# First attention layer: the norms of the first two batches by Sqrt on ScalarE and reciprocal on VectorE instead of powers on GpSimd, and the padded keys cleared by VectorE at the start

## The chip, the core and the metric

The kernel runs on one NeuronCore of one Trainium2 chip. The metric is the device time of one execution in microseconds (us); lower is better. TensorE (PE) multiplies matrices, ScalarE (ACT) evaluates activation functions, VectorE (DVE) and GpSimd (POOL) work elementwise, SyncE (SP) issues most of the transfers. Each engine runs its own instructions strictly in the order in which they were written down, and waits on semaphores for the others.

## What is computed

Four layers over a tensor x of 16 batches x 256 tokens x 128 features, each with its own layer norms and residual: an attention, a mixture of 8 experts, a second attention, and a mixture of 16 experts. The change touches the first attention alone. Cut to what matters:

```python
def _l2norm(x):                               # EPS_NORM = 1e-12
    n = jnp.linalg.norm(x, axis=-1, keepdims=True)
    return x / jnp.maximum(n, EPS_NORM)

x = layernorm(x) * ln_w + ln_b                # after an outer layernorm
q = _l2norm((x @ Wq + bq).reshape(B, S, 16, 8))
k = _l2norm((x @ Wk + bk).reshape(B, S, 16, 8))
v = (x @ Wv + bv).reshape(B, S, 16, 8)
state = q
for _ in range(2):
    sim = jnp.einsum('bqhd,bkhd->bqhk', state, k)
    state = jnp.einsum('bqhk,bkhd->bqhd', softmax(sim), v)
o = state.reshape(B, S, H) @ Wo + bo
return residual + o
```

The norm is taken over the 8 features of a head. With 128 tokens to a tile, 2 tiles to a batch, 16 heads, and q and k, a batch has 64 norms on each of the 128 partitions.

## The kernel before

`first_attention` is a software pipeline over steps k from -12 to 74. A unit is one group of four heads of one batch, so a batch b has the four units 4b to 4b+3, and 64 units make up the layer. In the code b is k // 4 and r is k % 4. Every engine's block walks through the same steps, and in each step writes down its share for several batches at once, each at another stage. Nothing schedules this but the order in the code and the semaphores. For one batch n the stages are these:

- k = 4n - 12 (r 0, b = n - 3): statistics of X on VectorE (`stats`, L617, and `moments`, L623), then their inverse root on GpSimd (`rstd` into `rs_a`: an addition at L801 and a power at L803).
- k = 4n - 11: the first normalisation into Z on VectorE (L604), the statistics of Z, and `rstd` again into `rs_b`.
- k = 4n - 10: the second normalisation into `z1` on VectorE (L604), its transposes on TensorE (L429), and `xT` on ScalarE (L575).
- k = 4n - 9 (r 3): the three projections of q, k and v on TensorE (L435, into two PSUM banks in turn), read on VectorE at L629 into `qk` and `vt`, and the squares `sq` (L736). On the same step `scaled` = `qk` times the inverse norms is made for the batch before (L671, in front of the reads), and ScalarE casts it into `qt` and `kt` (L565, L567).
- k = 4n - 8 (r 0): the sums of squares `ss` on VectorE (L705), the lower clip at 1e-24 on GpSimd (L852), and two of four powers of -0.5 on GpSimd into `rn` (`norm_powers`, L807, 16 of the 64 columns each).
- k = 4n - 7 (r 1): the other two powers, behind `rstd` of the next batch.
- k = 4n - 4 (r 0): GpSimd subtracts the rounded parts (L838, L840), which releases `stacks_ready`, and the steps 4n - 4 to 4n - 1 each transpose one unit's keys and queries (L423, task "KQ") and ScalarE copies them into `kq` (L590).
- k = 4n: the first unit of the batch is scored (L398), exponentiated on ScalarE (L539, two instructions of 128x1024 a step), and from step 4n + 1 on attended (L416), turned (L522), and worked on in VectorE for the second iteration, with row maxima (L409 on TensorE, L645 on VectorE).

So before step 0 there is nothing but this preparation of batches 0, 1 and 2, and from step 0 on the attention of one unit a step, beside the preparation of later batches.

`kpad`, a ring of four padded key tiles (128x4096 in all), is cleared once by GpSimd in step -6 (L865, at `FIRST + 6`). SyncE waits for that (`kpad_zero`) before its first small transfers into `kpad`, which also need the first copy into `kq`; the maxima first read `kpad` in step 3.

Of the kernel before, what the change touches and what calls it, by code (L numbers as in the profile page):

```python
# [16 lines left out]
F32 = mybir.dt.float32  # L17
F32R = mybir.dt.float32r
I32, U32 = mybir.dt.int32, mybir.dt.uint32
ALU = mybir.AluOpType  # L20
ACT = mybir.ActivationFunctionType
AX = mybir.AxisListType
# [3 lines left out]
B, S = 16, 256  # L26
TILES = B * S // P
TPB = S // P
H, HD = 16, 8
# [164 lines left out]
def first_attention(nc, X, Z, ident, a):  # L194
# [3 lines left out]
    FIRST, LAST = -3 * NG, UNITS + 3 * NG - 1  # L198
# [2 lines left out]
    D_ORDER = ("op", "m0", "qp", "m1", "m2", "lg", "place", "m3", "kp", "vp", "O")  # L201
    PEAK, TURN, SECOND, LAST_USE = 3, 4, 5, 6
    K_RING, Q_RING, PAD_RING, V_RING = NG + LAST_USE, NG + 1, 4, NG + LAST_USE + 1

    def steps(eng):
        for k in range(FIRST, LAST):
# [9 lines left out]
    def unit(n):  # L216
        return 0 <= n < UNITS

    def batch(n):
        return 0 <= n < B  # L220

    with ExitStack() as ctx:
# [6 lines left out]
        def sem(name):  # L229
            return ctx.enter_context(nc.semaphore("a0_" + name))  # L230
# [4 lines left out]
        sq = sb("sq", [P, 2, TPB, D])  # L235
        scaled = sb("scaled", [P, 2, TPB, D])
        ss = sb("ss", [P, 2 * TPB * H])
        rn = sb("rn", [P, 2 * TPB * H])
# [20 lines left out]
        kpad = sb("kpad", [P, PAD_RING, G, S], F32R)  # L259
# [22 lines left out]
        squares, norms, clipped, rn_ready = sem("squares"), sem("norms"), sem("clipped"), sem("rn_ready")  # L282
# [4 lines left out]
        set_up, pool_set_up, kpad_zero = sem("set_up"), sem("pool_set_up"), sem("kpad_zero")  # L287
        passed = a["passed"]
        route = sem("route")
        block = ctx.enter_context(nc.Block())  # L290


# [239 lines left out]
        def _(act):  # L532
# [15 lines left out]
            for st in steps(act):  # L548
                k = st.k
                b, r = k // NG, k % NG  # L550
                if unit(k):
                    exps(st, 0, k, p1)
                if a_live(k, "yT"):
# [40 lines left out]
        def _(dve):  # L594
            nc.vector.memset(mv_a[:, :, :], 1.0).then_inc(set_up, 1)
            nc.vector.memset(mv_b[:, :, :], 1.0).then_inc(set_up, 1)
            nc.vector.memset(qt2[:].rearrange("p a b c -> p (a b c)").bitcast(F32), 0.0).then_inc(set_up, 1)
            dve.wait_ge(set_up, 3)
            dve.wait_ge(a["loaded"], 16 * a["loads"])

# [32 lines left out]
            for st in steps(dve):  # L633
                k = st.k
# [12 lines left out]
                                            ALU.max, negate=True).then_inc(d_done, 1)  # L647


                if r == 3 and batch(b - 2):  # L650

                    dve.wait_ge(d_full, d_count(k, "op"))
                    dve.wait_ge(zb_ready, b - 1)
                    nc.vector.tensor_tensor(y[:].rearrange("p t d -> p (t d)"), narrow(k, "op"), Z[:, tiles(st, -2)],
                                            ALU.add).then_inc(d_done, 1)
# [41 lines left out]
                if r == 1 and batch(b - 3):  # L697
# [1 line left out]
                    dve.wait_ge(x_part, b - 2)  # L699
                    xx = X[:, tiles(st, -3)]  # L700
                    nc.vector.tensor_tensor(xx, xx, y[:].rearrange("p t d -> p (t d)"), ALU.add).then_inc(x_new, 1)
                if r == 0 and batch(b + 2):

                    dve.wait_ge(squares, b + 3)
                    nc.vector.tensor_reduce(ss[:, :], sq[:].rearrange("p a t (h d) -> p (a t h) d", d=HD), AX.X,  # L705
                                            ALU.add).then_inc(norms, 1)
# [84 lines left out]
        def _(pool):  # L791
# [18 lines left out]
            for st in steps(pool):  # L810
                k = st.k
# [32 lines left out]
                for g, (first, last) in enumerate(GROUPS[:-2]):  # L844
# [2 lines left out]
                        pool.wait_ge(route, ROUTE_SET_UP + ROUTE_LINKS * (g + 1))  # L847
                    if 0 <= part < 2 * (last + 1 - first) * TPB:
                        scatter(nc, Z, rt, first * TPB + part // 2, a["xs"], a["scattered"], (part % 2,))
                if r == 0 and batch(b + 2):  # L850
                    pool.wait_ge(norms, b + 3)
                    nc.gpsimd.tensor_scalar(ss[:, :], ss[:, :], 1e-24, None, ALU.max).then_inc(clipped, 1)  # L852
                    pool.wait_ge(clipped, b + 3)
                if r < 2 and batch(b + 2):
                    norm_powers(2 * r)
                    norm_powers(2 * r + 1)
                if k == FIRST + 3:
# [3 lines left out]
                    nc.gpsimd.memset(v32[:, :, :, :, HD].rearrange("p a b c -> p (a b c)"),  # L861
                                     1.0).then_inc(pool_set_up, 1)
                    pool.wait_ge(pool_set_up, 4)
                if k == FIRST + 6:
                    nc.gpsimd.memset(kpad[:].rearrange("p a b c -> p (a b c)").bitcast(F32), 0.0  # L865
                                     ).then_inc(kpad_zero, 1)


def second_attention(nc, X, Z, ident, a):
# [1601 lines left out]
```

## Time and profile before

| | |
|---|---|
| median of 3 runs | 1584.4 us (1583.03 to 1585.36) |
| the profiled execution | 1585.79 us, its span 1584.0 us |
| granted TensorE clock, mean | 0.934 of full speed |
| TensorE matmul busy | 1346.2 us (85%) |
| VectorE busy | 1132.1 us (71%) |
| ScalarE busy | 963.9 us (61%) |
| GpSimd busy | 771.9 us (49%) |

The span runs from the first to the last instruction of the core. Busy times are sums over all four layers, and matmuls are pipelined, so the share of TensorE says little of any one stretch; the first stretch is looked at by itself in the views that follow. Shapes are partitions x elements per partition.

### The profile page before, as it was taken

The page shows a single profiled execution, that of the slowest core. Times are in us where ns is not written, and L with a number is a line of the kernel's source. Part 1 is how long each engine was busy: PE and PEld are TensorE (multiplying, and loading weights), DVE is VectorE, ACT ScalarE, POOL GpSimd, SP SyncE. Part 2 cuts the span into 40 slices and gives each one's busy share as a digit, 9 for nine tenths or more (in the row PEclk, how much of TensorE's full clock was granted, in tenths as well). Part 3 has the DMA queues.
Part 4 walks back from the last instruction along what each step waited for, and adds up shares of the span by engine and source line. Part 5 has one row for each costly group of instructions (what it writes and reads, how often), then busy time and mean ns, then how long its engine had stood idle before and what let it go on. Part 6 is the DMA issues. An engine that isn't in the chain of part 4 may idle for free. (4 is left out here: it accounts for less than half of the span.)

```text
span 1584.0 us, 34293 instructions
## 1 busy us (share of the span) xinstructions
PE 1346.2 (85%) x12185; PEld 1024.2 (65%) x12185; DVE 1132.1 (71%) x3064; ACT 963.9 (61%) x1493; POOL 771.9 (49%) x976
## 2 busy tenths in 40 slices
PE   1699999999987677999338999899999997699997
PEld 1356666666654466999326777676777774588886
DVE  3378889888776455999636688678777876466766
ACT  0488888888875354777304666667666775343332
POOL 7966666777733344999554333444344321001111
PEclk9999999999998698999758999989999999699999
DMA  6010000111110120222202111111111110000000
GB/s 212 14 24 20 21 21 22 27 31 30 32 34 22 37 64 14 75 72 70 89 23 57 37 43 43 44 42 42 41 40 42 38 41 13 1 1 14 7 14 20
DMA packets 75101, 60.68 MB, mean 38 GB/s; under 512 B 17088, under 2 KB 71104, under 8 KB 74560
## 3 DMA queue, kind: packets, MB, share of 16 engines
q1 hardware_dynamic: 70848, 50.21, 11.8%
q0 software_dynamic: 4096, 8.40, 1.7%
q8 instruction: 95, 1.56, 0.4%
q14 instruction: 62, 0.51, 0.1%
HBM read 20.01 MB, written 13.37 MB: 21 GB/s over the span
## 5 line engine op out<-in xcount | busy, mean ns | idle before, releaser
L539 ACT ACTIVATE a_p<-a_ps_s 128x1024 f32<-128x1024 f32 x256 | 258.6, 1032 | 25.6 <-PE a_ps_s L398 23.0
L1263 DVE TENSOR_REDUCE a_qt<-a_ps_d 128x2 fp32r<-128x512 f32 x256 | 174.0, 690 | 73.8 <-PE a_ps_d L1062 40.6
L645 DVE TENSOR_REDUCE a_qt<-a_ps_d 128x2 fp32r<-128x512 f32 x256 | 174.7, 688 | 46.5 <-PE a_ps_d L409 40.3
L807 POOL TENSOR_TENSOR a_rn<-a_ss,a_half 128x16 f32<-128x16 f32 x64 | 186.1, 2924 | 1.5
L1062 PE MATMUL a_ps_d<-a_kpad,a_qs 128*128 128x512 f32 x256 | 126.4, 496 | 27.7 <-DVE a_qt L1263 19.7
L1175 ACT ACTIVATE a_pg<-a_ps_s 128x1024 f32<-128x1024 f32 x128 | 125.9, 1026 | 30.7 <-PE a_ps_s L1051 29.1
L416 PE MATMUL a_ps_o<-a_p,a_v 128*32 128x256 f32 x2048 | 129.3, 392 | 3.7 <-ACT a_p L539 3.7
L409 PE MATMUL a_ps_d<-a_kpad,a_qs 128*128 128x512 f32 x256 | 126.7, 495 | 3.1 <-DVE a_qt L645 2.3
L2195 ACT ACTIVATE f_s<-f_ps_g 128x512 f32<-128x512 f32 x72 | 43.0, 599 | 97.4 <-PE f_ps_g L2133 89.1
L416 PEld LDWEIGHTS a_ps_o<-a_p,a_v 128*32 128x32 f32 x2048 | 61.0, 112 | 53.3 <-issue 22.5
L1040 PE MATMUL a_ps_a<-ident,a_qt 128*128 128x128 f32 x512 | 84.8, 292 | 2.7 <-ACT a_kc L1193 1.2
L1958 DVE TENSOR_TENSOR f_sl<-f_s,f_sh 128x512 fp32r<-128x512 f32 x78 | 77.9, 1038 | 8.9 <-ACT f_sh L1846 8.9
L1062 PEld LDWEIGHTS a_ps_d<-a_kpad,a_qs 128*128 128x128 f32 x256 | 48.3, 190 | 54.6 <-DVE a_qt L1263 23.2
L190 POOL DMA_INDIRECT xs<-Z,r_at x64 | 68.2, 1066 | 24.2 <-issue 15.5
L1197 ACT CAST a_qsm<-a_ps_a 128x512 fp32r<-128x512 f32 x64 | 37.6, 587 | 62.5 <-PE a_ps_a L1040 62.5
L409 PEld LDWEIGHTS a_ps_d<-a_kpad,a_qs 128*128 128x128 f32 x256 | 48.1, 188 | 39.1 <-issue 11.6
L1040 PEld LDWEIGHTS a_ps_a<-ident,a_qt 128*128 128x128 f32 x512 | 66.5, 151 | 8.3 <-issue 6.5
L1452 POOL DMA_INDIRECT a_picked<-ys,rows x64 | 62.8, 981 | 17.7 <-issue 17.7
L1112 PE MATMUL a_ps_o<-a_pg,a_v 128*32 128x256 f32 x1024 | 68.5, 385 | 0.4 <-ACT a_pw L1201 0.4
L2244 DVE TENSOR_TENSOR f_p<-f_h,f_ps_x 128x512 f32<-128x512 f32 x64 | 43.8, 685 | 34.3 <-PE f_ps_x L2105 33.2
L2118 PEld LDWEIGHTS f_ps_y<-wd,f_p 128*128 128x128 f32 x512 | 65.3, 191 | 4.1 <-DVE f_p L2244 0.4
L2118 PE MATMUL f_ps_y<-wd,f_p 128*128 128x128 f32 x512 | 66.3, 275 | 0.2 <-DVE f_p L2244 0.2
(353 smaller groups left out, 3913.6 us busy)
## 6 DMA issues: line engine op xcount, KB each, us to landing
a_kpad<-a_kc SPq DMA_DIRECT2D x512, 32.0 KB
a_kpad<-a_kq SPq DMA_DIRECT2D x256, 32.0 KB, 1.8
f_xin<-xs SPq DMA_DIRECT2D x39, 128.0 KB, 2.1
ys<-f_yout SPq DMA_DIRECT2D x39, 128.0 KB, 2.1
w<-in_w SPq DMA_DIRECT2D x2, 2304.0 KB, 11.4
out_x<-X SPq DMA_DIRECT2D x8, 256.0 KB, 2.3
xs<-f_zero SPq DMA_DIRECT2D x15, 128.0 KB
wgu<-in_wgu SPq DMA_DIRECT2D x1, 1152.0 KB, 5.7
```

The costliest lines, as they stand in the source:

```text
L409: nc.tensor.matmul(bank(st.k, f"m{part}")[:, :], qs2[:, (st.k - 1) % 2, t * P:(t + 1) * P], kpad[:, u % PAD_RING, 2 * c:2 * c + 2, :].rear ...
L416: last = nc.tensor.matmul(ps_o[SLOT * j:SLOT * (j + 1), half * S:(half + 1) * S], v32[:, u % V_RING, t, j, :], probs[:, u % 2, j, t, :], s ...
L539: nc.scalar.activation(probs[:, u % 2, 2 * c:2 * c + 2, :, :].rearrange("p a b c -> p (a b c)"), ps_s[:, 2 * c:2 * c + 2, :].rearrange("p ...
L645: nc.vector.tensor_reduce(qt2[:, (k - PEAK) % 4, 2 * part:2 * part + 2, SHIFT], bank(k, f"m{part}")[:, :].rearrange("p (a b) -> p a b", b= ...
L807: nc.gpsimd.tensor_tensor(rn[:, part * c:(part + 1) * c], ss[:, part * c:(part + 1) * c], half[:, 0:c], ALU.pow).then_inc(rn_ready, 1)
L1040: last = nc.tensor.transpose(ps_a[:, n:n + P], stacked(src[:, (u // NG) % 2, kind, t * H + t0:t * H + t0 + G, :]), ident[:, :])
L1062: nc.tensor.matmul(bank(k, f"m{part}")[:, :], qs[:, k % 2, t * P:(t + 1) * P], kpad[:, k % PAD_RING, GLOBAL, 2 * c:2 * c + 2, :].rearrange ...
L1112: nc.tensor.matmul(ps_o[SLOT * j:SLOT * (j + 1), 0:S], v32[:, u % V_RING, t, j, :], pg[:, u % 2, j, t, :], start=t == 0, stop=t == TPB - 1)
L1175: nc.scalar.activation(pg[:, u % 2, 2 * c:2 * c + 2, :, :].rearrange("p a b c -> p (a b c)"), ps_s[:, 2 * c:2 * c + 2, :].rearrange("p a b ...
L1263: nc.vector.tensor_reduce(qt[:, b % 2, GLOBAL, n:n + 2, SHIFT], bank(k, f"m{part}")[:, :].rearrange("p (j s) -> p j s", s=S), AX.X, ALU.ma ...
L1958: nc.vector.tensor_tensor(sl[:, half_of(n, h)], s[:, half_of(n, h)], sh[:, half_of(n, h)].bitcast(F32), ALU.subtract).then_inc(sl_done, 1)
L2118: last = nc.tensor.matmul(ps_y[:, t * D:(t + 1) * D], src, a["wd"][:, q * D:(q + 1) * D], start=q == 0 and t == 0, stop=q == NQ - 1 and t ...
```

## The change

A constant `ROOTED = 2` names how many batches take the new way. For batches 0 and 1:

- VectorE makes the sums of squares at the very front of step 4n - 8 (before, they stood behind the statistics of the next batch), and clips them itself.
- ScalarE takes the square root in the same step, in place in `ss`.
- VectorE takes the reciprocal into `rn` at the front of step 4n - 7, and adds 4 to `rn_ready` at once.
- GpSimd does neither the clip nor the four powers.

Batches 2 to 15 keep the powers. Besides, `kpad` is cleared by VectorE in its set-up, behind the memset of `qt2`, and no longer by GpSimd.

```diff
+    ROOTED = 2
...
+        roots = sem("roots")
...
             for st in steps(act):
                 k = st.k
                 b, r = k // NG, k % NG
+                if r == 0 and 0 <= b + 2 < ROOTED:
+                    act.wait_ge(clipped, b + 3)
+                    nc.scalar.activation(ss[:, :], ss[:, :], ACT.Sqrt).then_inc(roots, 1)
                 if unit(k):
                     exps(st, 0, k, p1)
...
             nc.vector.memset(qt2[:].rearrange("p a b c -> p (a b c)").bitcast(F32), 0.0).then_inc(set_up, 1)
+            nc.vector.memset(kpad[:].rearrange("p a b c -> p (a b c)").bitcast(F32), 0.0).then_inc(kpad_zero, 1)
             dve.wait_ge(set_up, 3)
...
+                if r == 0 and 0 <= b + 2 < ROOTED:
+                    dve.wait_ge(squares, b + 3)
+                    nc.vector.tensor_reduce(ss[:, :], sq[:].rearrange("p a t (h d) -> p (a t h) d", d=HD), AX.X,
+                                            ALU.add).then_inc(norms, 1)
+                    dve.wait_ge(norms, b + 3)
+                    nc.vector.tensor_scalar(ss[:, :], ss[:, :], 1e-24, None, ALU.max).then_inc(clipped, 1)
+                if r == 1 and 0 <= b + 2 < ROOTED:
+                    dve.wait_ge(roots, b + 3)
+                    nc.vector.reciprocal(rn[:, :], ss[:, :]).then_inc(rn_ready, 4)
                 if r == 3 and batch(b - 2):
...
-                if r == 0 and batch(b + 2):
+                if r == 0 and ROOTED <= b + 2 < B:
 
                     dve.wait_ge(squares, b + 3)
...
-                if r == 0 and batch(b + 2):
+                if r == 0 and ROOTED <= b + 2 < B:
                     pool.wait_ge(norms, b + 3)
...
-                if r < 2 and batch(b + 2):
+                if r < 2 and ROOTED <= b + 2 < B:
                     norm_powers(2 * r)
                     norm_powers(2 * r + 1)
...
-                if k == FIRST + 6:
-                    nc.gpsimd.memset(kpad[:].rearrange("p a b c -> p (a b c)").bitcast(F32), 0.0
-                                     ).then_inc(kpad_zero, 1)
```

How the order of the instructions changes, at three places. The line numbers of the changed kernel are a little higher than those of the kernel before; the tiles are the same, named a_ for this layer.

GpSimd, from step -8 to step -4, before:

```order
L852 TENSOR_SCALAR a_ss<-a_ss 128x64 [waits a0_norms]
L807 TENSOR_TENSOR a_rn<-a_ss,a_half 128x16 [waits a0_clipped]
L807 TENSOR_TENSOR a_rn<-a_ss,a_half 128x16
L801 TENSOR_SCALAR a_ve<-a_mv_b 128x4 [waits a0_stats_b]
L803 TENSOR_TENSOR a_rs_b<-a_ve,a_half 128x4 [waits a0_pool_ve]
L807 TENSOR_TENSOR a_rn<-a_ss,a_half 128x16 x2
L865 MEMSET a_kpad 128x4096
L833 TENSOR_TENSOR Z<-Z,bo 128x256 [waits a0_z1_ready]
L824 COPY a_v<-a_vt 128x8x8 [waits a0_d_done]
L838 TENSOR_TENSOR a_qt<-a_scaled,a_qt 128x32x8 [waits a0_parts_hi]
L840 TENSOR_TENSOR a_kt<-a_scaled,a_kt 128x32x8
```

and with the change, from the same `rstd` of batch 1 (the power into `rs_a`) to the same end:

```order
L818 TENSOR_TENSOR a_rs_a<-a_ve,a_half 128x4 [waits a0_pool_ve]
L816 TENSOR_SCALAR a_ve<-a_mv_b 128x4 [waits a0_stats_b]
L818 TENSOR_TENSOR a_rs_b<-a_ve,a_half 128x4 [waits a0_pool_ve]
L848 TENSOR_TENSOR Z<-Z,bo 128x256 [waits a0_z1_ready]
L839 COPY a_v<-a_vt 128x8x8 [waits a0_d_done]
L853 TENSOR_TENSOR a_qt<-a_scaled,a_qt 128x32x8 [waits a0_parts_hi]
L855 TENSOR_TENSOR a_kt<-a_scaled,a_kt 128x32x8
```

The clip, four powers and the memset are gone, so that the `rstd` into `rs_b` and the subtractions into `qt` and `kt` follow each other directly.

VectorE, the end of step -9 and the steps -8 and -7, before:

```order
L629 TENSOR_TENSOR a_vt<-a_ps_d,bqkv 128x256 [waits a0_d_full]
L617 BN_STATS a_bn<-X 128x6 [waits x_first]
L617 BN_STATS a_bn<-X 128x6
L623 BN_AGGR a_mv_a<-a_bn 128x2 [waits a0_bn_done]
L623 BN_AGGR a_mv_a<-a_bn 128x2
L705 TENSOR_REDUCE a_ss<-a_sq 128x64 [waits a0_squares]
L604 TENSOR_SCALAR Z<-X,a_mv_a,a_rs_a 128x128 [waits a0_rs_a_ready]
```

and with the change:

```order
L635 TENSOR_TENSOR a_vt<-a_ps_d,bqkv 128x256 [waits a0_d_full]
L658 TENSOR_REDUCE a_ss<-a_sq 128x64 [waits a0_squares]
L661 TENSOR_SCALAR a_ss<-a_ss 128x64 [waits a0_norms]
L623 BN_STATS a_bn<-X 128x6 [waits x_first]
L623 BN_STATS a_bn<-X 128x6
L629 BN_AGGR a_mv_a<-a_bn 128x2 [waits a0_bn_done]
L629 BN_AGGR a_mv_a<-a_bn 128x2
L664 RECIPROCAL a_rn<-a_ss 128x64 [waits a0_roots]
L610 TENSOR_SCALAR Z<-X,a_mv_a,a_rs_a 128x128 [waits a0_rs_a_ready]
```

The sums of squares of batch 0 and their clip now stand ahead of the statistics of batch 1, and the reciprocal ahead of its first normalisation. The same pattern comes once more for batches 1 and 2, in steps -4 and -3.

ScalarE, from the first `xT` (step -10) to the Sqrt of batch 1 (step -4), with the change (before, the second load and both rows on `a_ss` are not there):

```order
L580 ACT_TABLE_LOAD [waits a0_a_full]
L580 ACTIVATE a_xT<-a_ps_a,ln_b,ln_w 128x256 [waits loaded]
L555 ACT_TABLE_LOAD
L555 ACTIVATE a_ss<-a_ss 128x64 [waits a0_clipped]
L580 ACTIVATE a_xT<-a_ps_a,ln_b,ln_w 128x256 [waits a0_a_full]
L570 CAST a_qt<-a_scaled 128x32x16 [waits a0_qk_scaled]
L572 CAST a_kt<-a_scaled 128x64x8
L555 ACTIVATE a_ss<-a_ss 128x64 [waits a0_clipped]
```

ScalarE around step 0, before:

```order
L590 CAST a_kq<-a_ps_a 128x2x256 [waits a0_a_full]
L565 CAST a_qt<-a_scaled 128x32x16 [waits a0_qk_scaled]
L567 CAST a_kt<-a_scaled 128x64x8
L590 CAST a_kq<-a_ps_a 128x2x256 [waits a0_a_full]
L539 ACTIVATE a_p<-a_ps_s 128x1024 [waits a0_scores_full] x2
L590 CAST a_kq<-a_ps_a 128x2x256 [waits a0_a_full]
```

and with the change:

```order
L570 CAST a_qt<-a_scaled 128x32x16 [waits a0_qk_scaled]
L572 CAST a_kt<-a_scaled 128x64x8
L595 CAST a_kq<-a_ps_a 128x2x256 [waits a0_a_full]
L541 ACT_TABLE_LOAD
L541 ACTIVATE a_p<-a_ps_s 128x1024 [waits a0_scores_full] x2
L595 CAST a_kq<-a_ps_a 128x2x256 [waits a0_a_full]
```

A table load now stands between the last copy into `kq` of step -1 and the first exponentials. It is the last one in this layer.

## Rows read from the trace of the kernel before

**Rows 1.** Windows: length; busy us (instructions) of PE, PEld, DVE, ACT, POOL; clock; DMA, GB/s.

```profile
30.00:40.00 10.00, 3.69 (x14) 2.71 (x12) 3.78 (x10) 1.71 (x3) 10.00 (x7) 1.00 0.00 0
...
80.00:120.00 40.00, 37.58 (x394) 23.07 (x395) 31.40 (x97) 33.78 (x47) 28.28 (x25) 1.00 0.10 24
```

**Rows 2.** Waits from 0 to 90 us: waiting, releaser, us in total, times, longest.

```profile
DVE a_z L604 <- POOL a_rs_b L803: 17.0, 4, 6.6
```

**Rows 3.** GpSimd's timeline: start, us, line, operation, idle before.

```profile
21.77 5.80 POOL L807 TENSOR_TENSOR a_rn<-a_ss,a_half 128x16 f32<-128x16 f32 x2
...
34.69 3.51 POOL L865 MEMSET a_kpad<- 128x4096 f32 x1
...
39.02 0.72 POOL L838 TENSOR_TENSOR a_qt<-a_scaled,a_qt 128x256 fp32r<-128x256 f32 x1
```

**Rows 4.** VectorE's timeline, the same columns.

```profile
9.11 0.60 DVE L604 TENSOR_SCALAR Z<-X,a_mv_a,a_rs_a 128x128 f32<-128x128 f32 x2 [1.57 <-POOL a_rs_a L803]
...
12.00 0.60 DVE L604 TENSOR_SCALAR a_z<-Z,a_mv_b,a_rs_b 128x128 f32<-128x128 f32 x2 [1.48 <-POOL a_rs_b L803]
...
18.59 0.42 DVE L629 TENSOR_TENSOR a_vt<-a_ps_d,bqkv 128x256 f32<-128x256 f32 x1
...
19.60 0.65 DVE L705 TENSOR_REDUCE a_ss<-a_sq 128x64 f32<-128x512 f32 x1
21.23 0.62 DVE L604 TENSOR_SCALAR Z<-X,a_mv_a,a_rs_a 128x128 f32<-128x128 f32 x2 [0.98 <-POOL a_rs_a L803]
...
29.04 0.60 DVE L604 TENSOR_SCALAR a_z<-Z,a_mv_b,a_rs_b 128x128 f32<-128x128 f32 x2 [6.39 <-POOL a_rs_b L803]
...
49.78 0.60 DVE L604 TENSOR_SCALAR a_z<-Z,a_mv_b,a_rs_b 128x128 f32<-128x128 f32 x2 [6.58 <-POOL a_rs_b L803]
...
58.51 0.42 DVE L629 TENSOR_TENSOR a_vt<-a_ps_d,bqkv 128x256 f32<-128x256 f32 x1 [0.77 <-PE a_ps_d L435]
...
69.08 0.60 DVE L604 TENSOR_SCALAR a_z<-Z,a_mv_b,a_rs_b 128x128 f32<-128x128 f32 x2 [2.54 <-POOL a_rs_b L803]
```

**Rows 5.** TensorE's timeline, the same columns.

```profile
15.41 2.96 PE L435 MATMUL a_ps_d<-wqkv,a_xT 128*128 128x128 f32 x12 [2.00 <-ACT a_xT L575]
...
31.05 2.08 PE L435 MATMUL a_ps_d<-wqkv,a_xT 128*128 128x128 f32 x8 [0.66 <-ACT a_xT L575]
...
40.48 0.69 PE L423 MATMUL a_ps_a<-ident,a_kt 128*128 128x128 f32 x2 [3.28 <-POOL a_kt L840]
...
52.75 1.92 PE L435 MATMUL a_ps_d<-wqkv,a_xT 128*128 128x128 f32 x8
...
57.74 0.63 PE L423 MATMUL a_ps_a<-ident,a_kt 128*128 128x128 f32 x2
...
67.09 1.94 PE L416 MATMUL a_ps_o<-a_p,a_v 128*32 128x256 f32 x16
69.74 0.45 PE L429 MATMUL a_ps_a<-ident,a_z 128*128 128x128 f32 x2 [0.71 <-DVE a_z L604]
```

**Rows 6.** ScalarE's timeline at the first exponentials, the same columns.

```profile
58.84 0.59 ACT L590 CAST a_kq<-a_ps_a 128x512 fp32r<-128x512 f32 x1 [1.45 <-PE a_ps_a L423]
59.59 1.94 ACT L539 ACTIVATE a_p<-a_ps_s 128x1024 f32<-128x1024 f32 x2 [0.16 <-PE a_ps_s L398]
```

**Rows 7.** ScalarE's timeline in the last layer, where the tables change.

```profile
1441.54 1.28 ACT L2202 ACT_TABLE_LOAD   x1
1442.83 0.26 ACT L2202 ACTIVATE f_ex<-f_lg 128x64 f32<-128x64 f32 x1
```

**Rows 8.** VectorE's groups by form: count, busy, mean ns, idle before.

```profile
L1966 DVE RECIPROCAL f_g<-f_den 128x32 f32<-128x32 f32 x1 | 0.4, 352 | 0.0
```

**Rows 9.** VectorE's timeline at the very start: the memset, the first statistics.

```profile
1.09 0.91 DVE L597 MEMSET a_qt<- 128x1024 f32 x1 [0.17 <-issue]
6.77 0.49 DVE L617 BATCH_NORM_STATS2 a_bn<-X 128x6 f32<-128x128 f32 x2 [4.77 <-DMA ln_b<-in_ln_b]
```

**Rows 10.** One window of 1 us, the columns of Rows 1.

```profile
74.00:75.00 1.00, 1.00 (x12) 0.39 (x8) 0.18 (x1) 1.00 (x2) 1.00 (x3) 0.50 0.00 0
```

## The prediction

> **What bounds the kernel now.** I read the windows first, to see where the time is not work. From 30 to 40 us TensorE is busy 3.7 us and GpSimd all 10; from 80 to 120 us TensorE is busy 37.6 of 40 [rows 1]. So the layer has a start in which TensorE mostly waits, and then a steady part in which it is the bound. The inputs are no limit in between: from 30 to 40 us the transfers move nothing (0 GB/s, [rows 1]), so the rest of X has landed before 30. Nothing later depends on a time of its own, so what the start loses, the whole program should lose.
>
> Then the waits up to 90 us: VectorE waits 17.0 us in four times for the inverse roots that GpSimd makes for the second normalisation [rows 2]. GpSimd's timeline shows why: the powers of one batch take 5.8 us a pair, in the same queue as the short `rstd` of the next batch. The `rstd` of batch 1 has to wait until the first pair ends at 27.57 [rows 3], though the statistics that it needs follow the normalisation of 21.23 at once; VectorE idles 6.39 us and normalises at 29.04 [rows 4]. The clearing of `kpad` (3.5 us at 34.69) delays the subtractions of step -4 in the same manner [rows 3]. Each batch of the preparation therefore takes about 20 us: the second normalisations come at 29.04, 49.78 and 69.08, where the reader sees GpSimd named as the releaser each time [rows 4].
>
> TensorE's timeline, last, shows what that does to it: keys are first transposed at 40.48, and the fourth unit's, after which the first scores can be made, at 57.74 [rows 5].
>
> **The change, step by step.** I follow the path with the powers gone, using lags of the same trace where nothing stood in the way. Times are from the span's start.
>
> Unimpeded lags: first to second normalisation, 9.11 to 12.00, is 2.9 us [rows 4]. From the first projection of batch 0 (15.41) to the read of v (18.59) is 3.2 us, and its 12 matmuls take 3.0 without a break [rows 4, 5].
>
> Step A, batch 1 reaches TensorE. VectorE now puts the sums of squares (0.65 us [rows 4]) and the clip (64 columns; I put it at 0.2, a little under the 0.26 of ScalarE's 64 columns [rows 7]) ahead of batch 1's statistics: +0.9. Its first normalisation moves from 21.23 to 22.1, its second comes 2.9 later at 25.0, and no longer at 29.04. That is -4.0 [rows 4].
>
> Step B, batch 0's keys. ScalarE's Sqrt waits for the clip until about 19.9, and all that stands behind it on ScalarE is the next `xT` at 26.4. Its table load carries no wait and runs right after the first `xT`, before 17, where ScalarE has nothing else to do. The reciprocal of 64 columns I estimate at 0.55 us, from 0.35 for 32 columns [rows 8], so the norms stand at 21 and `scaled` no longer waits. The projections start at 27.0 (31.05 less 4.0) and run their 3.0 us through, to 30.0, because both banks are read in time [rows 5]. The two casts behind `xT` (0.6 us each, as the cast into `kq` [rows 6]) end at 28.1, and the two subtractions (0.7 each [rows 3]) at 29.6, since GpSimd has nothing else to do. So the first transposes of keys come at 30.0 and not at 40.48: -10.5 [rows 5]. ScalarE's second Sqrt, in front of the first copy into `kq`, holds that copy about 0.7 us; only the copy and the second transposes feel it, and they have 4 us of slack before the `xT` of batch 2.
>
> Step C, batch 2. v of batch 1 is read from 30.2; 18.59 to 21.23 and the 0.9 make 3.5 us to the first normalisation, 2.9 more to the second: 36.6 and not 49.78, -13.2 [rows 4].
>
> Step D, to the last of the first four transposes. Before, projections began 3.0 after the second normalisation (52.75 against 49.78), then stood while `scaled` waited for the norms, and the transposes came at 57.74 [rows 4, 5]. Now it is 36.6 + 3.0 + 3.0 = 42.5: -15.2. GpSimd's subtractions for batch 1 follow the casts of 40.4 and end at about 43.0, before TensorE asks for them, behind the first scores, at 44.4.
>
> Step E, the table. The exponentials would start at 59.59 - 15.2 = 44.4. Now a table load stands behind the copy into `kq` that ends at 59.43 - 15.2 = 44.2 [rows 6]. In the last layer a load takes 1.28 us and the ACTIVATE follows 0.01 us later [rows 7]. So they start at 45.5: the gain here is 14.1.
>
> Step F, where two paths meet. Batches 2 and 3 still go the old way. v of batch 2 is read 3.2 after its projections start, from 42.8, and was read from 58.51 [rows 4], so all that hangs on GpSimd from there moves by 15.8: the second normalisation of batch 3 from 69.08 to 53.3 [rows 4]. But TensorE, which follows the exponentials, ends the attending that began at 67.09 at 67.09 + 1.94 - 14.1 = 55.0, and only then transposes `z1`, at 55.0 and not at 69.74 [rows 5]. Before, TensorE waited 0.71 us here; this wait hides most of the table load. From there TensorE is nearly gapless: **the gain is 14.7 us**.
>
> At nothing: the clearing of `kpad` on VectorE. By 0.91 us for 1024 columns [rows 9] its 4096 take some 3.6 us, from 2.0 to 5.6, and VectorE stands idle until 6.77 for the loads of inputs [rows 9]; the cover has 1.2 us to spare, and a memset twice as slow would cost 2.4. Nothing for `kpad_zero` either: SyncE needs the first `kq` copy as well. Both reciprocals cost nothing either: each runs while VectorE would wait for `rstd`'s result. The same goes for GpSimd's lost work, once it is off the path.
>
> Bounds of the unknown costs. Sqrt and reciprocal are not in this layer's trace; with 0.26 to 1.0 us each they stay inside the 5 us between the clip and `scaled` of batch 0, and inside a similar gap for batch 1, so both ends are nothing. The load's effect lies between 0 (all hidden) and 1.3, which sets the gain between 14.1 and 15.4; I take 0.7, by the meeting in step F. TensorE's clock is the larger unknown. It is granted half (1.2 of 2.4 GHz) at 74 to 75 us [rows 10], after a stretch in which TensorE was idle in several short waits, the one of 0.71 at 69.74 among them [rows 5]. The new start has other gaps, so such a stretch may be missing or come once more. I put it at 1.7 us either way, half of an attending, scores and maxima at the slow level (the 1.94 us of 67.09 and about as much again [rows 5]).
>
> The sum by the profiled execution is 1585.8 - 14.7 = 1571.1; it lies 1.4 above the median, and from the median the forecast is 1584.4 - 14.7 = **1569.7 us**.
>
> **A rule that speaks against it.** The rows show a table load of 1.28 us, an idle gap of 0.01 us behind it, and 0.26 for a small ACTIVATE [rows 7]. The Trainium skill (ScalarE: Activation LUTs, section What ACT_TABLE_LOAD costs) counts about 1.38 us of drain on top, 2.66 in all for each switch. By that the gain would be 13.3 and the time 1571.1; the trace does not bear the drain out.
>
> **The rivals.** (a) A switch of tables costs its engine more than the load. Then ScalarE, and TensorE behind it, are 1.4 us later at step 0: 1571.1. For it: the first exponentials follow a copy without a pause, as in no row before. Against: rows 7.
> (b) The gain is given back in steps 0 to 4: batch 2 still has its powers, two pairs of 5.8 us and an `rstd` between them, and if GpSimd holds the pace there, TensorE only waits longer. For it: batch 3's second normalisation waited 2.54 us for GpSimd [rows 4]. Against: that work starts from v of batch 2, which moves by 15.8, more than TensorE does. If half of the gain went, 1577.
> (c) The change doesn't do what it says: the norms were not what held the start, and the second normalisation waits for something else (the loads of X or weights). Then it saves only the 3.5 us of `kpad` at most: 1581 to 1584. Against: the releaser of each long wait is GpSimd, with its queue full of powers [rows 2 to 4].
> (d) Slower: the new phase of TensorE's gaps keeps its clock at half in the steady part. There it is busy 37.6 of 40 us [rows 1], so each microsecond of that work costs one more at half clock. From 15 us of such work on the gain is gone, and the whole 40 us at half clock give 1569.7 + 37.6 = 1607. It decides at the first stretch after step 3, where the clock last fell to 0.50 [rows 10].
>
> **How the numbers follow.** The forecast gets 0.80, (a) 0.09, (b) 0.06, (c) 0.03, (d) 0.02. The forecast with clock (1.7 either way), the load's bounds and the 1.4 between runs spans about 1566 to 1573; (a) reaches 1574.2. The range is 1566.0 to 1574.5. Some 0.2% (3.2 us) is what a measurement of this kernel can tell from no change. Faster by more: forecast, (a), (b), and half of (c), 0.965; within: the other half of (c), 0.015; slower: (d), 0.02.
>
> **What the profile would show.** The second normalisations at 25.0, 36.6 and 53.3; first keys transposed at 30.0; a load of 1.28 at 44.2 and exponentials at 45.5; the first wait on `scaled` gone. From 80 us on, every row of before should stand about 14.7 earlier, and the second to fourth layers should take what they took. A first statistics row after 6.8 would show the memset uncovered; a shift that shrinks between steps 0 and 6 would show (b). A clock other than 0.50 and 1.00 in turn at other places would account for the last 2 us.

## The result, and the profile after

The kernel before took 1583.72 us (median of 4 runs, 1580.65 to 1585.36), the changed one 1567.38 us (4 runs, 1564.52 to 1570.1): a ratio of 0.9899, with an interval of 0.9872 to 0.9925. That is 16.3 us less, or 12 to 20 by the interval; forecast were 14.7 less and 1569.7 us. The profiled execution took 1570.1 us against 1585.8, its span is 1568.3 us, 15.7 less, and its mean granted clock 0.935 against 0.934.

The windows of the changed kernel come first. Columns: stretch, its length, busy time of TensorE, its weight loads, VectorE, ScalarE and GpSimd with counts, granted clock, DMA share, GB/s. The second row is the stretch of 80 to 120 us of [rows 1], moved by 16.

```profile
30.00:40.00 10.00, 4.05 (x17) 2.90 (x16) 4.76 (x17) 2.45 (x6) 4.38 (x9) 1.00 0.11 27
64.00:104.00 40.00, 37.61 (x397) 22.90 (x397) 30.92 (x96) 34.20 (x47) 28.78 (x25) 1.00 0.10 23
```

From 30 to 40 us GpSimd is busy 4.4 us where it was busy all 10, and the steady part is as full as before (37.61 of 40).

The waits of the first 75 us (engine and line, who was waited for; total us, times, longest):

```profile
PE a_ps_a L431 <- DVE a_z L610: 23.5, 3, 12.5
POOL a_ve L816 <- DVE a_mv_a L629: 14.4, 5, 4.6
DVE a_z L610 <- POOL a_rs_b L818: 5.5, 4, 1.5
```

The third row answers to [rows 2]: VectorE waited 17.0 us for the second inverse root and now waits 5.5, never longer than 1.5, which is about the length of that small step itself (an addition of 0.23 us and a power of 1.04). The direction has turned: GpSimd now waits for VectorE's statistics.

GpSimd's timeline of the changed kernel (start, length), to be read against [rows 3]:

```profile
23.61 1.04 POOL L818 TENSOR_TENSOR a_rs_b<-a_ve,a_half 128x4 f32<-128x4 f32 x1
25.36 1.10 POOL L848 TENSOR_TENSOR Z<-Z,bo 128x256 f32<-128x256 f32 x1 [0.72 <-DVE a_z L610]
...
27.73 0.73 POOL L853 TENSOR_TENSOR a_qt<-a_scaled,a_qt 128x256 fp32r<-128x256 f32 x1 [1.09 <-ACT a_kt L572]
28.42 0.73 POOL L855 TENSOR_TENSOR a_kt<-a_scaled,a_kt 128x256 fp32r<-128x256 f32 x1
...
45.43 5.80 POOL L822 TENSOR_TENSOR a_rn<-a_ss,a_half 128x16 f32<-128x16 f32 x2
51.17 0.24 POOL L839 COPY a_v<-a_vt 128x64 f32<-128x64 f32 x1
51.50 0.23 POOL L816 TENSOR_SCALAR a_ve<-a_mv_b 128x4 f32<-128x4 f32 x1
51.82 1.04 POOL L818 TENSOR_TENSOR a_rs_b<-a_ve,a_half 128x4 f32<-128x4 f32 x1
```

The powers appear for the first time at 45.43, for batch 2; from there the old pattern is back, with the `rstd` of batch 3 behind a pair of 5.80 us.

VectorE's timeline of the changed kernel; the bracket is the idle time before the row and its releaser:

```profile
2.80 3.47 DVE L603 MEMSET a_kpad<- 128x4096 f32 x1 [0.80 <-issue]
6.53 0.48 DVE L623 BATCH_NORM_STATS2 a_bn<-X 128x6 f32<-128x128 f32 x2 [0.26 <-DMA ln_b<-in_ln_b]
...
19.38 0.20 DVE L661 TENSOR_SCALAR a_ss<-a_ss 128x64 f32<-128x64 f32 x1
...
20.17 0.52 DVE L664 RECIPROCAL a_rn<-a_ss 128x64 f32<-128x64 f32 x1
...
24.68 0.60 DVE L610 TENSOR_SCALAR a_z<-Z,a_mv_b,a_rs_b 128x128 f32<-128x128 f32 x2 [1.48 <-POOL a_rs_b L818]
25.20 0.68 DVE L686 TENSOR_TENSOR a_scaled<-a_qk,a_rn 128x512 f32<-128x512 f32 x1
...
36.15 0.67 DVE L610 TENSOR_SCALAR a_z<-Z,a_mv_b,a_rs_b 128x128 f32<-128x128 f32 x2 [1.48 <-POOL a_rs_b L818]
...
52.89 0.60 DVE L610 TENSOR_SCALAR a_z<-Z,a_mv_b,a_rs_b 128x128 f32<-128x128 f32 x2 [1.10 <-POOL a_rs_b L818]
```

Against [rows 4] the second normalisations of batches 1, 2 and 3 went from 29.04, 49.78 and 69.08 to 24.68, 36.15 and 52.89. `scaled` follows the normalisation with no wait. The clearing of `kpad` ends at 6.27, and 0.26 us later the inputs let the statistics start.

ScalarE at its switch of tables, the timeline of the changed kernel:

```profile
42.94 0.59 ACT L595 CAST a_kq<-a_ps_a 128x512 fp32r<-128x512 f32 x1 [1.89 <-PE a_ps_a L425]
43.54 1.28 ACT L541 ACT_TABLE_LOAD   x1
44.84 1.94 ACT L541 ACTIVATE a_p<-a_ps_s 128x1024 f32<-128x1024 f32 x2
```

TensorE's timeline of the changed kernel, against [rows 5]:

```profile
29.51 0.63 PE L425 MATMUL a_ps_a<-ident,a_kt 128*128 128x128 f32 x2
41.84 0.64 PE L425 MATMUL a_ps_a<-ident,a_kt 128*128 128x128 f32 x2
52.34 1.56 PE L418 MATMUL a_ps_o<-a_p,a_v 128*32 128x256 f32 x16
53.84 0.44 PE L431 MATMUL a_ps_a<-ident,a_z 128*128 128x128 f32 x2
...
57.60 1.07 PE L418 MATMUL a_ps_o<-a_p,a_v 128*32 128x256 f32 x16
...
63.90 0.50 PE L400 MATMUL a_ps_s<-a_kq 32*128 32x256 f32 x8
```

The attending that begins at 67.09 in [rows 5] begins here at 52.34, 14.75 earlier. It takes 1.56 instead of 1.94, and the transposes of `z1` follow it without the 0.71 of idle time. The scores of step 4 (last row) started at 80.38 before:

```profile
80.38 0.51 PE L398 MATMUL a_ps_s<-a_kq 32*128 32x256 f32 x8
```

**What becomes of it later.** From trace to trace the scores of step 4 come 16.5 us earlier, VectorE's last row maxima of the layer 16.0, the first SiLU of the second layer 14.3 and of its last stretch 12.8, the second attention's first exponentials 12.3 and its last 15.6, the end 15.7. So the shift wanders between 12.3 and 16.5 us and ends at 15.7. Where it shrinks, in the second layer, the clock was lower (windows of 550 to 590 us before, then 534 to 574 after):

```profile
550.00:570.00 20.00, 14.96 (x68) 11.93 (x67) 14.24 (x33) 9.55 (x11) 13.42 (x12) 0.91 0.30 89
570.00:590.00 20.00, 16.72 (x81) 13.33 (x82) 9.25 (x15) 12.01 (x16) 5.02 (x6) 1.00 0.12 37
```
```profile
534.00:554.00 20.00, 16.04 (x70) 13.01 (x69) 12.22 (x31) 8.99 (x11) 12.56 (x13) 0.83 0.27 82
554.00:574.00 20.00, 16.37 (x71) 12.62 (x70) 10.82 (x15) 12.89 (x17) 6.06 (x6) 0.91 0.14 43
```

### The profile page after: what moved, and what is told of

It is laid out like the page before. It is cut to its first block and busy times, and to the rows that moved or that the text cites. A ratio compares the mean times of both kernels' runs of the same rounds, so it can differ in the third digit from the quotient of the medians.

```text
span 1568.3 us, 34293 instructions
## 1 busy us (share of the span) xinstructions
PE 1340.1 (85%) x12185; PEld 1019.2 (65%) x12185; DVE 1136.0 (72%) x3069; ACT 965.1 (62%) x1497; POOL 745.2 (48%) x965
## 3 DMA queue, kind: packets, MB, share of 16 engines
q8 instruction: 95, 1.56, 0.4%
## 5 line engine op out<-in xcount | busy, mean ns | idle before, releaser
L822 POOL TENSOR_TENSOR a_rn<-a_ss,a_half 128x16 f32<-128x16 f32 x56 | 162.8, 2924 | 1.3
L1187 ACT ACTIVATE a_pg<-a_ps_s 128x1024 f32<-128x1024 f32 x128 | 125.8, 1024 | 27.0 <-PE a_ps_s L1063 25.4
L418 PEld LDWEIGHTS a_ps_o<-a_p,a_v 128*32 128x32 f32 x2048 | 61.0, 112 | 53.1 <-issue 22.3
L1970 DVE TENSOR_TENSOR f_sl<-f_s,f_sh 128x512 fp32r<-128x512 f32 x78 | 77.3, 1030 | 8.3 <-ACT f_sh L1858 8.3
```

Of the source, the lines that this page charges most:

```text
L418: last = nc.tensor.matmul(ps_o[SLOT * j:SLOT * (j + 1), half * S:(half + 1) * S], v32[:, u % V_RING, t, j, :], probs[:, u % 2, j, t, :], s ...
L822: nc.gpsimd.tensor_tensor(rn[:, part * c:(part + 1) * c], ss[:, part * c:(part + 1) * c], half[:, 0:c], ALU.pow).then_inc(rn_ready, 1)
L1187: nc.scalar.activation(pg[:, u % 2, 2 * c:2 * c + 2, :, :].rearrange("p a b c -> p (a b c)"), ps_s[:, 2 * c:2 * c + 2, :].rearrange("p a b ...
L1970: nc.vector.tensor_tensor(sl[:, half_of(n, h)], s[:, half_of(n, h)], sh[:, half_of(n, h)].bitcast(F32), ALU.subtract).then_inc(sl_done, 1)
```

## The experiments

They ran on three other chips (called the first, second and third chip here), where the kernel before takes 1523.8, 1523.8 and 1525.9 us. The change itself was run on the second and the third of them and gives nearly the ratio of above. All times are compared within one chip, and places in a profile are given net of the few tenths by which inputs landed at other times, where that is said. Diffs are against the changed kernel unless the text says otherwise.

**The two executions to compare with.** On the second chip the changed kernel and the one before were run as they are.

> The change once more, for TensorE's clock. If the last 1.7 us of the start's gain come from clock levels that fall by chance, the granted clock at 55 to 60 us differs in this profile (a stretch at 0.50) and the scores of step 4 come up to 1.7 us later than 63.90, at up to 65.6; if they come from the change itself, 63.9 again.

> The kernel before once more, for TensorE's clock. If the fall to 0.50 at 72.6 to 76.0 us is chance, it stands elsewhere or is missing here, and the scores of step 4 come up to 1.7 us earlier or later than 80.38; if it belongs to the kernel, it stands at the same place.

The changed kernel took 1507.6 us (ratio 0.9891, 0.9873 to 0.991), the one before 1523.72 (0.9999). The gain is 16.2 us (1523.77, the kernel before as it ran beside this one, less 1507.6). The steps repeat within 0.05 us up to 52.86, the second normalisation of batch 3. Then they part: the scores of step 4 start at 66.34 here, 0.7 later than the latest that I expected (65.6), and at 63.90 in the first profile. The windows show where the clock differs (first the changed kernel's first profile, then this one; the clock stands third from the end):

```profile
56.00:58.00 2.00, 1.82 (x21) 1.20 (x25) 0.72 (x5) 1.19 (x3) 2.00 (x1) 1.00 0.00 0
```
```profile
56.00:58.00 2.00, 1.87 (x11) 1.17 (x14) 0.84 (x5) 0.50 (x2) 2.00 (x1) 0.50 0.00 0
60.00:62.00 2.00, 2.00 (x17) 1.11 (x9) 0.02 (x1) 1.85 (x4) 0.59 (x3) 0.50 0.00 0
```

One kernel, two executions: the granted clock of 0.50 ended at 53.4 us in one and at 63.1 in the other. The kernel before is no different: 0.50 from 72.6 to 76.0 us in its first profile, from 63.7 to 77.3 in this one, and its scores of step 4 start at 81.51 and not at 80.38. Between these two profiles of the second chip the scores of step 4 gain 81.51 − 66.34 = 15.2 us, where the first pair of traces says 16.5.

**The norms alone** (first chip). `kpad` is cleared by GpSimd again, behind step -6, as before the change:

```diff
-            nc.vector.memset(kpad[:].rearrange("p a b c -> p (a b c)").bitcast(F32), 0.0).then_inc(kpad_zero, 1)
...
+                if k == FIRST + 6:
+                    nc.gpsimd.memset(kpad[:].rearrange("p a b c -> p (a b c)").bitcast(F32), 0.0
+                                     ).then_inc(kpad_zero, 1)
```

> The norms go the new way, kpad is cleared by GpSimd in step -6 again. Theory: with the powers gone, the 3.5 us of clearing fall into GpSimd's idle time before the casts of batch 0 (24.7 to 28.2); the first key transposes come at about 30.7 instead of 29.51, and this vanishes in TensorE's wait for the second normalisation of batch 2 at 36.15. Scores of step 4 at 63.9 as with the whole change, and the whole gain of about 16 us. Rival (the two edits add up): 3.5 us later everywhere, scores of step 4 at 67.4, and a gain of 12 to 13.

1509.78 us, ratio 0.9902 (0.9885 to 0.9918): 14.0 us less than the kernel before on this chip, so the norms bring most of the gain alone. But the batches were late, and not in the way that I expected. GpSimd's row and then VectorE's of this kernel's timeline:

```profile
24.54 3.51 POOL L879 MEMSET a_kpad<- 128x4096 f32 x1
```
```profile
24.62 3.58 DVE L609 TENSOR_SCALAR a_z<-Z,a_mv_b,a_rs_b 128x128 f32<-128x128 f32 x2 [1.47 <-POOL a_rs_b L817]
```

GpSimd delayed nothing in its own queue that mattered. The two normalisations, started 0.08 us behind the memset, took 3.58 us instead of 0.60: they ended at 28.20, and the memset at 28.05. Batch 2's second normalisation came at 39.04 instead of 36.15, 2.9 late, and the scores of step 4 at 66.78 instead of 63.90, where 63.9 was expected. The transfers are not the reason: they move 442 GB/s from 24 to 26 us in the changed kernel as in this one, and there the two normalisations take 0.60.

**`kpad` alone** (first chip; `ROOTED = 0`, so that all norms are GpSimd's powers).

> Only the clearing of kpad moves to VectorE, all norms by powers (ROOTED = 0). Theory: GpSimd reaches the rstd of batch 2 at 38.3 and not at 40.39, so everything from there is 2.1 to 2.3 us earlier: second normalisation of batch 2 at 47.6 instead of 49.78, scores of step 4 at about 78.2 instead of 80.38, time 1581.5. Rivals: the full 3.5 us; or nothing, if the clearing was hidden.

1522.07 us, ratio 0.9989 (0.9977 to 1.0002): not to be told from no change. The second normalisation of batch 2 is at 48.77, 0.85 earlier than in the kernel before as it ran on the second chip (49.62), or 1.5 net of inputs that landed 0.6 later, where 2.1 was expected. Part of what is missing is on one row, where VectorE now scales beside GpSimd's addition of `bo` and takes 1.20 instead of 0.69 us:

```profile
35.16 0.72 POOL L848 TENSOR_TENSOR Z<-Z,bo 128x256 f32<-128x256 f32 x1
35.23 1.20 DVE L686 TENSOR_TENSOR a_scaled<-a_qk,a_rn 128x512 f32<-128x512 f32 x1 [5.13 <-POOL a_rn L822]
```

**One batch instead of two** (first chip; `ROOTED = 1`).

> ROOTED = 1: only batch 0 by square root, batch 1 by powers again. Theory: batch 1's two pairs of powers stand in front of the second normalisation of batch 2 (about 40.3 instead of 36.15) and of scaled of batch 1 (about 46.1 instead of 36.73); first exponentials at about 51.2 instead of 44.84, scores of step 4 near 70.4, time 6.5 us above the whole change (about 1574). Rival (only the first batch is on the path, the second's powers are covered): as the whole change, scores of step 4 at 63.9.

1513.24 us, ratio 0.9926 (0.991 to 0.9943). VectorE's timeline of this kernel shows the two waits of the kernel before again, that of the normalisation (6.58 in [rows 4]) and that of `scaled` (5.13, in front of the row at 34.78):

```profile
40.63 0.60 DVE L610 TENSOR_SCALAR a_z<-Z,a_mv_b,a_rs_b 128x128 f32<-128x128 f32 x2 [6.57 <-POOL a_rs_b L818]
46.37 0.70 DVE L686 TENSOR_TENSOR a_scaled<-a_qk,a_rn 128x512 f32<-128x512 f32 x1 [5.13 <-POOL a_rn L822]
```

Expected were 40.3 and 46.1, exponentials at 51.2 (measured 51.59) and the scores of step 4 at 70.4 (70.48). In time 6.5 us above the whole change were expected; its three ratios (0.9878 to 0.9899) put this run 4 to 7 us above it. Each of the first two batches counts, and the reckoning by lags holds for a second kernel.

**Three batches** (second chip; `ROOTED = 3`).

> ROOTED = 3: batch 2 by square root as well. Theory: GpSimd's powers no longer hold the second normalisation of batch 3 nor scaled of batch 2 (the wait of 1.82 us at 58.63 goes), while the Sqrt of batch 2 now stands in front of the exp table load and pushes the first exponentials by about 0.4 us. Scores of step 4 at about 63.4 (0.5 earlier), time within 1 us of the whole change. Rival (the powers of batch 2 are the bound of steps 2 and 3): 1.5 to 2 us earlier.

1508.53 us, ratio 0.9897 (0.988 to 0.9915). Both waits on GpSimd in batch 3's path are gone, the second normalisation comes at 52.09 and `scaled` at 57.93. Yet the scores of step 4 start at 66.64, against 66.34 in the changed kernel on this chip, where 0.5 us earlier was expected. So the powers of batch 2, which make VectorE wait 1.00 us before `scaled` in the changed kernel on this chip, bound nothing here. Both of these profiles have the clock at 0.50 there. In the first profile, with 1.00, the wait is 1.82, and TensorE then idles 0.67 us (to 59.98) for the row maxima that follow `scaled`; that these powers cost nothing at the higher clock is not shown.

**The exponentials' table earlier** (second chip). A dummy `Exp` behind the last square root loads the table in ScalarE's idle time.

```diff
+                    if b + 2 == ROOTED - 1:
+                        nc.scalar.activation(spare[:, :], a["ln_w"][:, 0:1], ACT.Exp)
```

> The whole change with one extra Exp of 128x1 right behind the second Sqrt, so that the exp table is loaded at 31 us in ScalarE's idle time and not at step 0. Theory (step F): the first exponentials come 1.2 us earlier (43.6 instead of 44.84), but batch 2's powers hold the second normalisation of batch 3 at 52.9 and scaled at 58.6, so the scores of step 4 move by 0.3 us at most and the time by nothing that can be measured. Rival: the load is wholly on the path, scores of step 4 at 62.7 and 1.2 us less.

1508.24 us, ratio 0.9895 (0.9878 to 0.9912): no gain that shows. ScalarE's timeline of this kernel:

```profile
31.53 1.28 ACT L558 ACT_TABLE_LOAD   x1
...
42.89 1.95 ACT L542 ACTIVATE a_p<-a_ps_s 128x1024 f32<-128x1024 f32 x2
```

The exponentials start 1.9 us earlier than in the unchanged copy (44.79), where 1.2 was expected. VectorE's row for batch 3 does not move, and its wait for GpSimd grows to 3.74:

```profile
53.00 0.60 DVE L613 TENSOR_SCALAR a_z<-Z,a_mv_b,a_rs_b 128x128 f32<-128x128 f32 x2 [3.74 <-POOL a_rs_b L821]
```

The transposes of `z1` start right behind it, at 53.66, which is 0.5 us earlier than in the unchanged copy (54.16) and not 1.9. So batch 3 hides most of the load, and what is left is too little to show in the time. The scores of step 4 start at 65.26 against 66.34, within the scatter of the clock.

**A longer set-up** (third chip). VectorE clears `kpad` twice, the second time behind the first.

```diff
+            nc.vector.memset(kpad[:].rearrange("p a b c -> p (a b c)").bitcast(F32), 0.0).then_inc(set_up, 1)
+            dve.wait_ge(set_up, 4)
```

> The whole change with kpad cleared twice by VectorE before the first statistics (the second behind the first by a wait). Theory: the first statistics start at 9.8 instead of 6.53, everything slips by 3.3 us and the end with it: second normalisation of batch 2 at 39.5, time 3.3 us above the whole change on the same chip. Rival (the start has slack against the later stages): less than 1 us in the time.

> The change a third time, as the base for the three others on the same chip and for the clock. Up to the first scores (42.8) the instructions stand within 0.3 us of the first two profiles (apart from when the inputs land); the scores of step 4 between 63.9 and 66.4, according to where the granted clock is 0.50 between 46 and 64 us.

The changed kernel took 1506.99 us here (ratio 0.9878, 0.986 to 0.9895), this one 1510.37 (0.9904, 0.9887 to 0.9921). VectorE's timeline of the longer set-up:

```profile
7.18 3.47 DVE L605 MEMSET a_kpad<- 128x4096 f32 x1 [0.92 <-DMA ln_b<-in_ln_b]
10.57 0.42 DVE L625 BATCH_NORM_STATS2 a_bn<-X 128x6 f32<-128x128 f32 x2
```

The first statistics are 4.0 us late (10.57 against 6.57), the second normalisation of batch 2 is 3.9 late (40.11 against 36.20), and the whole kernel 3.4 by the medians; no run of the one is as fast as the slowest of the other. The two profiled executions are only 1.9 apart, and already 2.0 at the scores of step 4 (67.85 against 65.88), since the clock of 0.50 ended at about 58 us in the one and at 62.4 in the other. So a delay of the start is paid nearly in full, against the rival's less than 1 us. This also prices an uncovered clearing of `kpad` on VectorE: about its 3.47 us.

The unchanged copy has its first scores at 42.44, 0.4 us before the 42.8 that I expected within 0.3, and those of step 4 at 65.88, inside the 63.9 to 66.4.

**GpSimd clears `kpad` early** (third chip), right behind its own set-up of v, where it is idle.

> As the norms-only kernel, but GpSimd clears kpad in step -9, right behind the clearing of v32 (about 15.9 to 19.4 us), where VectorE reads PSUM and squares. Theory (the 2.9 us of the norms-only kernel come from GpSimd's memset holding up VectorE's two normalisations of 128x128 that ran beside it, 3.58 instead of 0.60 us): nothing runs in that form there, so the second normalisation of batch 1 takes 0.60 us at about 24.7, that of batch 2 comes at 36.2, as with the whole change, and the time is the same as its. Rival (a memset of 3.5 us in GpSimd's queue costs about 3 us wherever it stands before step -4): batch 2's at 39.0.

1507.79 us, ratio 0.9879 (0.9861 to 0.9897), the change's own time. The memset runs from 16.94 to 20.45, and the second normalisation of batch 1 takes its 0.60. That of batch 2 comes at 37.11, or 36.1 net of inputs that landed 1.0 later, as expected. So the delay is not that of a memset in GpSimd's queue wherever it stands, and VectorE is no better place for it than GpSimd; what counts is that no such normalisation runs beside it.

**Four pieces** (third chip): the norms alone, but GpSimd clears `kpad` in four memsets of 1024 columns.

> As the norms-only kernel, with GpSimd's memset of 128x4096 in step -6 cut into four of 128x1024 (about 0.9 us each). Theory (VectorE is held until the GpSimd instruction in flight ends): the pair of normalisations at 24.7 takes 0.9 to 1.8 us and not 3.58, and batch 2's second normalisation comes at 36.5 to 37.5. Rival (VectorE gets no turn while GpSimd has memsets to stream): 3.5 us and 39.0, as in one piece.

1510.07 us, ratio 0.9895 (0.9878 to 0.9912). The pieces and the normalisations of this kernel's timeline:

```profile
24.73 0.95 POOL L880 MEMSET a_kpad<- 128x1024 f32 x1
25.62 0.95 POOL L880 MEMSET a_kpad<- 128x1024 f32 x1
26.51 1.99 POOL L880 MEMSET a_kpad<- 128x1024 f32 x2
```
```profile
24.81 2.79 DVE L609 TENSOR_SCALAR a_z<-Z,a_mv_b,a_rs_b 128x128 f32<-128x128 f32 x2 [1.48 <-POOL a_rs_b L817]
```

Neither expectation holds. VectorE did not get in behind the first piece, which ended near 25.6, nor did it wait for all four (28.5). It came through at 27.6, and the last piece alone took 1.09 instead of 0.95. Why it had to let three pieces pass stays open.

## Why the prediction was right

**Steps A to D** stood within 0.7 us and erred to one side:

| place | forecast | measured |
|---|---|---|
| second normalisation, batch 1 | 25.0 | 24.68 |
| first transposes of keys | 30.0 | 29.51 |
| second normalisation, batch 2 | 36.6 | 36.15 |
| transposes of the fourth unit | 42.5 | 41.84 |
| table load, exponentials | 44.2, 45.5 | 43.54, 44.84 |
| second normalisation, batch 3 | 53.3 | 52.89 |
| transposes of `z1` | 55.0 | 53.84 |

Of each difference 0.24 us is the inputs, which landed earlier (statistics at 6.53, not 6.77). Some sums of the prediction are 0.1 off by rounding (36.6 + 3.0 + 3.0 is 42.6, 58.51 less 42.8 is 15.7, 67.09 + 1.94 − 14.1 is 54.9), which changes nothing. The clip of 0.20 and the reciprocal of 0.52 were put at 0.2 and 0.55. The run with one batch shows these steps as causes and not only as coincidence, since giving batch 1 alone its powers back brings back the waits of 6.57 and 5.13 within 0.4 us of the places worked out.

**Step E**: the load takes 1.28 us and the exponential follows 0.02 later, so rival (a) with its drain falls here too. The Trainium skill (ScalarE: Activation LUTs, What ACT_TABLE_LOAD costs) counts some 1.38 us more; the trace shows none of it.

**Step F** had the mechanism right: the load meets batch 3 and is mostly hidden. The run with the early `Exp` shows 0.5 us of it left at the transposes of `z1`, where the forecast had 0.7. The place of these transposes was 1.2 us off, 55.0 against 53.84: 0.66 came from step E, 0.38 from an attending that took 1.56 and not 1.94. Up to step 4 came another 0.6, for 16.5 in all; in that stretch an attending took 1.07 (57.60) where one took 1.94 in the kernel before (73.72). This part is chance, since the same kernel showed 1.94 for both and 66.34 in another execution.

Not all of the surplus is chance. The gain was above 14.7 on each chip that had the change (16.3, 16.2 and 18.9 us by the medians), and between the two profiles of the second chip, with an attending of 1.93 and 1.94 in front of both, the transposes of `z1` moved by 69.56 − 54.16 = 15.4. The lags of steps A to D, each a few tenths too long, make about 0.5 of it. Where the rest of the third chip's 18.9 comes from stays open.

**The clock's term** was about right as a bound. I put 1.7 us either way around a gain of 14.7, so scores of step 4 at 64.0 to 67.4; three executions of the changed kernel have them at 63.90, 66.34 and 65.88. As forecasts of one execution from another such a bound is too narrow, for two of these differ by 2.4. Its price came from the attending of 67.09, whose 1.94 us I took as the half clock; the view has a granted clock of 1.00 there (see the last section).

**`kpad` at nothing** came out right by less than the text claimed. The length was right (3.47 against 3.6), but the row starts 0.80 us later than I let it, at 2.80, and the cover left is 0.26 us, not 1.2. What I did not see at all is the worth of the move. I followed the memset through GpSimd's queue only. Left there, with the norms changed, it runs beside batch 1's second normalisations and holds them, and batch 2 is 2.9 us late. In time it would be 0.5 to 3.7 us (ratio 0.9902, against the change's 0.9899, 0.9891 and 0.9878 on other chips); the intervals overlap and the two were not run on one chip, so the rows show the loss and the times only agree. On the third chip the four pieces, 2.3 late at batch 2 (38.47 against 36.20), cost 3.1 us. So beside the new norms the move pays because VectorE's normalisations are not held, and not because of GpSimd's queue.

**The later layers** did not "take what they took": the shift wandered between 12.3 and 16.5 and ended at 15.7. That it came back is not explained by the prediction.

**The rivals.** (b), the gain given back behind the powers of batch 2: the wait is there, but taking it away with three rooted batches gains nothing in time. (c) fell with the waits of 5.5 us and with the run of `kpad` alone, whose 1.7 us can't be told from nothing. (d) fell with a clock of 1.00 in the steady part and 0.935 in the mean.

No experiment beat the change on its chip. The best of them, the early memset on GpSimd and the early `Exp`, are 0.8 and 0.6 us above it, within the intervals.

## What to carry to other kernels

Where short operations on the critical path stand behind long ones in an engine's queue, moving the long ones away is worth the delay of the short ones, over every round in which it occurs, and not the busy time: here GpSimd lost 23.4 us of powers (8 of 2.92 each) and the kernel 16.3. It is worth that only while nothing else takes over as the bound: the third batch's move gained nothing. Lags of a round that nothing impeded price the new start well. Before an operation is moved, or others move beside it, look at what runs beside it on the engine that shares its way to memory, and not only at its queue, and look in a trace whether that neighbour holds it: a memset did, and the powers did not.

## What the runs showed of the hardware

**A GpSimd memset holds VectorE.** A write-only memset of 3.51 us on GpSimd kept two 128x128 fp32 normalisations for 3.58 instead of 0.60 us. The Trainium skill (SBUF — State Buffer, Who interferes with whom) says that GpSimd and VectorE share one pair of ports, which whoever starts first keeps for a whole instruction, that VectorE needs it in its two-port mode, which a `tensor_scalar` can take, or with two inputs in SBUF, and that in the second case it is in the way only of a GpSimd operation that reads. The traces agree in the cases that follow, and disagree in one. The normalisation waited for the memset. (That it ran in the two-port mode is the Trainium skill's account; no row names a mode.) `scaled`, a `tensor_tensor` with both inputs in SBUF, took 0.69 us in the kernel before although it began 0.09 behind that same memset:

```profile
34.78 0.69 DVE L671 TENSOR_TENSOR a_scaled<-a_qk,a_rn 128x512 f32<-128x512 f32 x1 [5.13 <-POOL a_rn L807]
```

It took 1.20 when it began 0.07 behind GpSimd's addition of `bo`, which reads. And when it began first, at 25.20 in the changed kernel, it took 0.68 and the addition 1.10 instead of 0.72. In the four pieces three memsets went past before the normalisations were through; why stays open.

The case that disagrees is the power. In the kernel before, a GpSimd power of 128x16, a `tensor_tensor` that reads and writes SBUF, starts 0.06 us in front of the same two normalisations for three batches in turn, and they take 0.60 each time (29.04, 49.78 and 69.08 in [rows 4]). The first of the three, from GpSimd's timeline of the kernel before:

```profile
28.98 5.77 POOL L807 TENSOR_TENSOR a_rn<-a_ss,a_half 128x16 f32<-128x16 f32 x2
```

So a GpSimd instruction that runs 2.9 us does not hold VectorE for its whole length whatever it is. What sets the power apart from the memset and the addition was not tried.

**Two chips, one kernel.** The kernel before takes 1583.7 us on one chip and 1523.8 to 1525.9 on three others. The start is the same within 1.2 us (scores of step 4 at 80.38 and 81.51), and most of the difference lies in the second attention, whose exponentials run for 487 us (846.4 to 1333.2) on the one and 437 (837.5 to 1274.9) on the other, at a mean granted clock of 0.95 and 1.00. The ratio of the change shows no dependence on it: 0.9899, 0.9891 and 0.9878, with overlapping intervals. Why the chips differ was not tried.

**The clock at a start.** Which stretch has a granted clock of 0.50 (1.2 of 2.4 GHz) differs between executions of one kernel, and how long it is: 3.4 and 13.6 us in two of the kernel before, 6.8 and 17.0 in two of the changed one, whose other rows agree within 0.05 us up to 52.86. Two executions of the changed kernel differ by up to 2.4 us at the scores of step 4.

The granted clock of the view is not the whole of TensorE's pace at a start. In the first profile of the kernel before it stands at 1.00 from 12 to 72 us, and yet the attendings of 62.40 and 67.09 take 1.94 us, as long as that of 73.72 at 0.50; that of 81.25 takes 1.07. In the second profile of the changed kernel it is 0.50 from 22.3 to 42.7 as well, where it is 1.00 in the first, and the twelve projections of batch 1 take 3.03 us in both. So at a start the pace is read from the rows of TensorE, and the granted clock beside it.
